# Zero matmuls ahead of the first load, a first load in halves, and a reordered first pair in an adaptive-norm FFN kernel with low-rank experts

## The reference

```python
W = weights[condition]                                  # (64 samples, 64, 64)
y = jnp.einsum('bct,bcd->bdt', x, W)                    # channels mixed per sample
logits = y @ gate_w.T                                   # 8 experts
w, sel = jax.lax.top_k(logits, 2); w = softmax(w)
result = y @ base_w.T + base_b                          # 1024 -> 1024
low    = y @ lora_A.T                                   # 8 experts of rank 16
result = result + 2.0 * sum_e(gate_e * low_e @ lora_B[e].T)
out = x + result
```

## Time and profile before

| what | value |
|---|---|
| median of the three runs | 504.84 us |
| the profiled execution's own time | 504.92 us |
| its span, first to last instruction | 502.8 us |
| PE busy | 489.8 us (97%) |
| DVE, ACT, POOL busy | 364.8, 380.7, 125.5 us |
| mean granted clock of PE | 0.997 |

### The profile page before, as it was taken

The page is one execution under the profiler, slowest core; times in us unless marked ns, Lnnn a source line. Parts: engine busy times, 40 slices in busy tenths (PEclk is TensorE's granted clock), DMA queues, the critical chain, the costliest instruction groups (busy, mean ns, idle before and its releaser), DMA issues.

```text
span 502.8 us, 8563 instructions
## 1 busy us (share of the span) xinstructions
PE 489.8 (97%) x2776; PEld 481.2 (96%) x2776; DVE 364.8 (73%) x768; ACT 380.7 (76%) x739; POOL 125.5 (25%) x111
## 2 busy tenths in 40 slices
PE   5979999999999999999999999999999999999997
PEld 5879999999999999999999999999999999999997
DVE  3987777877777877777877777877777877777654
ACT  4947887877887877887877887877887877887620
POOL 1240233321233320333311233321233321233110
PEclk9989999999999999999999999999999999999999
DMA  8812112222112222112222112222112222111112
GB/s 332 339 42 85 47 39 83 85 86 83 47 36 83 83 83 83 42 42 83 83 83 83 42 42 83 83 83 83 40 43 83 83 83 83 40 45 43 43 43 83
DMA packets 11105, 40.07 MB, mean 80 GB/s; under 512 B 1234, under 2 KB 1618, under 8 KB 11090
## 3 DMA queue, kind: packets, MB, share of 16 engines
q1 hardware_dynamic: 10946, 39.36, 21.6%
q10 hardware_dynamic: 144, 0.52, 0.3%
HBM read 23.10 MB, written 16.78 MB: 79 GB/s over the span
## 4 chain that ended last, share of the span: by engine, by line
PE 93%; DVE 3%; DMA 2%; ACT 1%; SPq 0%; issue 0%
PE acc L579 78%; PE acc L611 9%; PE mixed L599 6%; DMA w_raw<-in_proj_w 2%; DVE w_lo L408 2%; PE acc L605 1%; DVE ties L455 0%; ACT w_hi L308 0%; DVE x_parts L421 0%; DVE lb_lo L531 0%; DVE w_raw L429 0%; DVE y_lo L414 0%; SPq L201 0%; ACT cw_parts L362 0%; SPq L197 0%
## 5 line engine op out<-in xcount | busy, mean ns | idle before, releaser
L335 ACT COPY y_moved<-w_raw 32x256 f32<-32x256 f32 x480 | 194.2, 405 | 40.1 <-DVE w_raw L429 34.1
L579 PE MATMUL acc<-w_hi,y_hi 128*128 128x384 f32 (+1 forms) x768 | 182.8, 343 | 0.1
L579 PE MATMUL acc<-w_lo,y_hi 128*128 128x384 f32 (+1 forms) x768 | 179.9, 339 | 0.8 <-DVE w_lo L408 0.8
L579 PE MATMUL acc<-w_hi,y_lo 128*128 128x384 f32 (+1 forms) x768 | 179.6, 339 | 0.0
L268 POOL TENSOR_TENSOR w_raw<-x_sb,bias 128x1024 f32<-128x1024 f32 x32 | 77.1, 2410 | 350.9 <-DVE low L485 260.3
L579 PEld LDWEIGHTS acc<-w_hi,y_hi 128*128 128x128 f32 x768 | 136.0, 189 | 7.0 <-issue 0.4
L579 PEld LDWEIGHTS acc<-w_lo,y_hi 128*128 128x128 f32 x768 | 138.8, 188 | 1.9 <-DVE w_lo L408 1.8
L579 PEld LDWEIGHTS acc<-w_hi,y_lo 128*128 128x128 f32 x768 | 139.0, 188 | 0.1
L429 DVE TENSOR_TENSOR w_raw<-mixed,w_raw 64x1024 f32<-64x1024 f32 x60 | 73.0, 1216 | 40.5 <-ACT w_raw L327 40.1
L437 DVE STREAM_TRANSPOSE y_turned<-y_moved 128x512 f32<-128x512 f32 x60 | 39.2, 691 | 55.2 <-ACT y_moved L335 55.2
L421 DVE TENSOR_TENSOR x_parts<-x_sb,x_parts 64x1024 fp32r<-64x1024 f32 x60 | 74.0, 1234 | 1.9
(11 more groups left out here) (45 smaller groups left out, 240.1 us busy)
## 6 DMA issues: line engine op xcount, KB each, us to landing
x_sb<-in_x SPq DMA_DIRECT2D x32, 512.0 KB, 3.8
out<-w_raw SPq DMA_DIRECT2D x31, 512.0 KB, 2.9
w_raw<-in_proj_w SPq DMA_DIRECT2D x8, 580.0 KB, 9.6
cw<-in_cond_w ACTq DMA_DIRECT2D x1, 512.0 KB, 3.8
lb_raw<-in_lora_b SPq DMA_DIRECT2D x1, 512.0 KB, 14.4
bias<-in_base_b SPq DMA_DIRECT2D x1, 512.0 KB, 15.8
out<-w_raw SPq DMA_DIRECT2D x2, 192.0 KB, 1.9
out<-w_raw SPq DMA_DIRECT2D x1, 128.0 KB, 2.0
```

The source lines that it names most:

```text
L335: done = nc.scalar.copy(y_moved[q * SQ:(q + 1) * SQ, g, :, :], piece.rearrange("m (k q a) -> m q k a", q=QUARTERS, a=SQ)[:, q, :, :])
L579: return nc.tensor.matmul(acc[:, c % 2, b, 0:hi - lo], y_part[:, c % 2, k, :], w_part[:, k, lo:hi], start=(k == 0 and product == 0), stop= ...
```

## The change

Six edits. (1) POOL clears a tile `zeros`, and PE multiplies it with itself 8 times before it waits for x. (2) x of pair 0 is loaded in two halves with a semaphore each, and `mix_first(0, 0)` waits for the first half alone. (3) The register loads of the conditions of pairs 0 and 1 are made before the wait for `cw`; ACT rounds `cw` in halves as its first work, and the low part moves from POOL to DVE. (4) `w_high(0)` comes behind both `y_high_first` of pair 0 and covers 384 columns, DVE copies the other 776 (signal `w_first`). (5) In `first_step` the `w_lo` products run a block behind; in step 1 the mix of pair 2 moves from before k=0 to behind it, and its second half from behind k=1 to behind k=2; `lb_lo` moves from before the gates of pair 0 to behind `add_rest`. (6) POOL's `add_bias` in step c is that of pair c-1 instead of c, and the last is behind the steps.

The core of the diff:

```diff
-            load_x(0, 0)
+            sp.dma_start(x_sb[:, 0, 0:T // 2], x_pairs[0, :, 0:T // 2]).then_inc(x_first, 16)
+            sp.dma_start(x_sb[:, 0, T // 2:T], x_pairs[0, :, T // 2:T]).then_inc(x_in[0], 16)
...
@@ gpsimd
+            nc.gpsimd.memset(zeros[:, :], 0.0).then_inc(zeros_ready, 1)
...
-            pool.wait_ge(cw_hi_ready, 1)
-            nc.gpsimd.tensor_tensor(cw_parts[:, 1, :], cw[:, :], cw_parts[:, 0, :].bitcast(F32), ALU.subtract) \
-                .then_inc(cw_ready, 1)
-            pool.wait_ge(cw_ready, 1)
+            pool.wait_ge(cw_ready, 2)
             select(0, 2)
-            pool.wait_ge(w_ready, KT)
-            pool.wait_ge(lb_ready, 1)
             pool.wait_ge(bias_in, 16)
-            add_bias(0, 0)
             def step(j, c, ahead=True):
                 pool.wait_ge(low_ready, 4 * j + c)
-                add_bias(j, c)
+                add_bias(j, c - 1)
...
@@ scalar
-            w_high(0)
+            act.wait_ge(cw_in, 16)
+            for cols in CW_HALVES:
+                nc.scalar.copy(cw_parts[:, 0, cols], cw[:, cols]).then_inc(cw_hi_ready, 1)
             y_high_first(0, 0)
             y_high_first(0, 1)
+            w_high(0)
             w_high(1)
             w_high(2)
-            act.wait_ge(cw_in, 16)
-            nc.scalar.copy(cw_parts[:, 0, :], cw[:, :]).then_inc(cw_hi_ready, 1)
...
@@ vector
+            for i, cols in enumerate(CW_HALVES):
+                dve.wait_ge(cw_hi_ready, i + 1)
+                nc.vector.tensor_tensor(cw_parts[:, 1, cols], cw[:, cols], cw_parts[:, 0, cols].bitcast(F32),
+                                        ALU.subtract).then_inc(cw_ready, 1)
             y_low_first(0, 0)
+            dve.wait_ge(w_in[0], 16)
+            nc.vector.tensor_copy(w_hi[:, 0, BW:N], w_raw[:, 0, BW:N]).then_inc(w_first, 1)
...
@@ tensor, first_step
                 for k in range(KT):
                     pe.wait_ge(w_hi_ready, k + 1)
                     for b in range(3):
-                        project(0, k, b, 0)
-                    pe.wait_ge(w_ready, k + 1)
-                    for b in range(3):
-                        project(0, k, b, 1)
+                        if k == 0 and b == 1:
+                            pe.wait_ge(w_first, 1)
+                        project(0, k, b, 0, last=1)
...
+                        with_w_lo(0)
+                    if k >= 2:
+                        with_w_lo(k - 1)
+                with_w_lo(KT - 1).then_inc(proj_done, 1)
@@ tensor, step
-                if ahead:
+                if ahead and c >= 2:
                     mix(j, c + 1, 0)
...
-                    if k == 1 and ahead:
+                    if k == 0 and c == 1:
+                        mix(j, c + 1, 0)
+                    if k == (2 if c == 1 else 1) and ahead:
                         mix(j, c + 1, 1)
@@ tensor, start
-            pe.wait_ge(consts_ready, NE)
-            pe.wait_ge(x_in[0], 16)
+            pe.wait_ge(zeros_ready, 1)
+            for _ in range(WARM):
+                nc.tensor.matmul(acc[:, 1, 0, 0:P], zeros[:, :], zeros[:, :], start=True, stop=True)
+            pe.wait_ge(x_first, 16)
```

More of the change, by code:

```diff
@@ L85, in adaln_ffn_kernel @@
         ident = sb("ident", [P, P], F32)
+        zeros = sb("zeros", [P, P], F32)
         earlier = sb("earlier", [P, NE, NE], F32)
@@ L127, in adaln_ffn_kernel @@
         bias_in = sem("bias_in")
+        x_first = sem("x_first")
         x_in = [sem(f"x_in{i}") for i in range(4)]
@@ L134, in adaln_ffn_kernel @@
         lb_ready = sem("lb_ready")
+        zeros_ready = sem("zeros_ready")
         w_zero = sem("w_zero")
+        w_first = sem("w_first")
         first_lower = sem("first_lower")
@@ L190, in adaln_ffn_kernel @@
         LAST = PAIRS - 1
+        WARM = 8
+        CW_HALVES = (slice(0, CONDITIONS * CH // 2), slice(CONDITIONS * CH // 2, CONDITIONS * CH))
         @block.sync
@@ L245, in _ @@
                                     pattern=[[-1, P]], channel_multiplier=1).then_inc(consts_ready, 1)
[L247 to L251, removed]
             def select(j, c):
@@ L271, in _ @@
             pool.wait_ge(cond_in, 16)
+            lower = [pool.value_load(cond_sb[0:1, 2 * c:2 * c + 1], min_val=0, max_val=CONDITIONS - 1)
+                     for c in range(2)]
             pool.wait_ge(cw_in, 16)
             pool.wait_ge(w_zero, 1)
-            select_first(0)
-            select_first(1)
-            pool.wait_ge(cw_hi_ready, 1)
-            nc.gpsimd.tensor_tensor(cw_parts[:, 1, :], cw[:, :], cw_parts[:, 0, :].bitcast(F32), ALU.subtract) \
-                .then_inc(cw_ready, 1)
-            pool.wait_ge(cw_ready, 1)
+            for c in range(2):
+                nc.gpsimd.tensor_copy(w_pair[0:CH, c, 0:CH], cw[0:CH, bass.ds(lower[c] * CH, CH)]) \
+                    .then_inc(first_lower, 1)
+            pool.wait_ge(first_lower, 2)
+            pool.wait_ge(cw_ready, 2)
             select(0, 2)
-            pool.wait_ge(w_ready, KT)
-            pool.wait_ge(lb_ready, 1)
             pool.wait_ge(bias_in, 16)
-            add_bias(0, 0)
             def step(j, c, ahead=True):
                 pool.wait_ge(low_ready, 4 * j + c)
-                add_bias(j, c)
+                add_bias(j, c - 1)
                 if ahead:
                     select(j, c + 2)
-            for n in (1, 2, 3):
+            for n in (1, 2, 3, 4):
                 step(0, n)
             with pool.Fori(0, LOOPS) as j:
-                for u in (4, 5, 6, 7):
+                for u in (5, 6, 7, 8):
                     step(j, u)
-            for n in range(PAIRS - 4, PAIRS):
+            for n in range(PAIRS - 3, PAIRS):
                 step(0, n, ahead=(n + 2 < PAIRS))
+            add_bias(0, LAST)
         @block.scalar
@@ L307, in w_high @@
                 act.wait_ge(w_in[k], 16)
-                nc.scalar.copy(w_hi[:, k, :], w_raw[:, k, :]).then_inc(w_hi_ready, 1)
+                cols = slice(0, BW if k == 0 else N)
+                nc.scalar.copy(w_hi[:, k, cols], w_raw[:, k, cols]).then_inc(w_hi_ready, 1)
             def y_high_first(c, h):
@@ L510, in _ @@
             dve.wait_ge(cond_in, 16)
+            upper = [dve.value_load(cond_sb[0:1, 2 * c + 1:2 * c + 2], min_val=0, max_val=CONDITIONS - 1)
+                     for c in range(2)]
             dve.wait_ge(cw_in, 16)
@@ L513, in _ @@
             for c in range(2):
-                cond = dve.value_load(cond_sb[0:1, 2 * c + 1:2 * c + 2], min_val=0, max_val=CONDITIONS - 1)
-                nc.vector.tensor_copy(w_pair[CH:P, c, CH:P], cw[CH:P, bass.ds(cond * CH, CH)]).then_inc(first_upper, 1)
-            w_low(0)
+                nc.vector.tensor_copy(w_pair[CH:P, c, CH:P], cw[CH:P, bass.ds(upper[c] * CH, CH)]) \
+                    .then_inc(first_upper, 1)
+            for i, cols in enumerate(CW_HALVES):
+                dve.wait_ge(cw_hi_ready, i + 1)
+                nc.vector.tensor_tensor(cw_parts[:, 1, cols], cw[:, cols], cw_parts[:, 0, cols].bitcast(F32),
+                                        ALU.subtract).then_inc(cw_ready, 1)
             y_low_first(0, 0)
+            dve.wait_ge(w_in[0], 16)
+            nc.vector.tensor_copy(w_hi[:, 0, BW:N], w_raw[:, 0, BW:N]).then_inc(w_first, 1)
             y_low_first(0, 1)
-            for k in range(1, 4):
+            dve.wait_ge(w_first, 1)
+            for k in range(4):
                 w_low(k)
@@ L541, in step @@
                     add_rest(j, c + 1, 1)
+                if c == 1:
+                    dve.wait_ge(lb_hi_ready, 1)
+                    nc.vector.tensor_tensor(lb_lo[:, :], lb_raw[:, :], lb_hi[:, :].bitcast(F32), ALU.subtract) \
+                        .then_inc(lb_ready, 1)
                 if split:
@@ L574, in _, with project @@
             PRODUCTS = [(y_hi, w_hi), (y_hi, w_lo), (y_lo, w_hi)]
-            def project(c, k, b, product):
+            def project(c, k, b, product, last=2):
                 y_part, w_part = PRODUCTS[product]
@@ L579, in project @@
                 return nc.tensor.matmul(acc[:, c % 2, b, 0:hi - lo], y_part[:, c % 2, k, :], w_part[:, k, lo:hi],
-                                        start=(k == 0 and product == 0), stop=(k == KT - 1 and product == 2))
+                                        start=(k == 0 and product == 0), stop=(k == KT - 1 and product == last))
             def mix_first(c, h):
@@ L615, in first_step, with with_w_lo @@
             def first_step():
+                def with_w_lo(k):
+                    pe.wait_ge(w_ready, k + 1)
+                    for b in range(3):
+                        done = project(0, k, b, 1, last=1)
+                    return done
                 for k in range(KT):
@@ L627, in first_step @@
                     for b in range(3):
-                        done = project(0, k, b, 2)
+                        project(0, k, b, 2, last=1)
                     if k == 0:
@@ L693, in _ @@
             mix_first(0, 0)
+            pe.wait_ge(x_in[0], 16)
             mix_first(0, 1)
```

(1 more changed line is left out.)

4 lines of the change are left out of this document (removed).

## The result

| | median | runs | span of the profiled run |
|---|---|---|---|
| before | 504.95 us | 4 | 502.8 us |
| changed | 499.50 us (498.83 to 500.05) | 4 | 497.6 us |

The ratio is 0.9893, interval 0.9871 to 0.9915: 5.4 us faster. The forecast was 498.5 with a range of 497.1 to 500.7.

What follows compares the result with a forecast made beforehand. PE, busy 97% of the span, was taken as the bound, with at most 19 us to win. Gains of 2.3 + 4.1 = 6.4 us from 504.92 gave 498.5 us, own range 497.4 to 499.4, overall 497.1 to 500.7.

Steps and rivals of the forecast that it cites:

- Start: Edits 1 to 4, up to the first product: mix of pair 0 from 5.4 us, taking 1.95 instead of 3.54.
- The rival with the low clock: Mix of pair 0 stays at the low clock despite the zeros; gain 5.3 us, time 499.6, chance 0.18.
- The copy of 776 columns: DVE's share of weight block 0 before the first product: 0.85 us, costing 0.1 at most.
- First product: PE's first product of pair 0, forecast to start at 8.6 us, after ACT's w_hi of 384 columns ends at 8.5.
- The rival on splitting x: Halves of x delay the weights by at most 0.9 us, shifting DMA, ACT and DVE; time 499.4, chance 0.07.
- First step: Pair 0, with w_lo a block behind: ends at 23.35 us against 25.63, 2.3 us gained.
- Step 1 and 2: PE's 3.07 us wait in step 1 and its clock loss go: 5.0 less 0.9, so 4.1 us gained.
- The loss put in at 0.9: New lateness in steps 1 and 2, including a 0.5 us wait for lowT_lo; 0.9 us, bounds 0 and 2.
- The 5.0 us: What step 1 lost before the change by the wait and low clock: 20.14 us against 15.11.
- Bias a pair later: Edit 6 in steady steps: later loads of x and the extra add at the end cost nothing.

Runs made afterwards that it cites:

- x_whole: The changed kernel with x of pair 0 loaded in one transfer instead of two halves; 500.32 us, ratio 0.9919.
- repaired_whole: The kernel of repaired with x of pair 0 loaded in one transfer instead of two halves; 498.24 us, ratio 0.9878.
- bias_early: The changed kernel with POOL's bias additions back at their old places (pair c in step c); 500.58 us, ratio 0.9921.
- repaired: The changed kernel with weight block 0 rounded before pair 0's second y_high, x of pair 3 ahead of lb_raw, lowT_lo ahead of x_low in step 1; 499.24 us.
- after_again: The changed kernel run and profiled once more with nothing edited; 499.88 us, ratio 0.9903.

## Why the prediction was right, and where it was off

The measured 499.50 lies in the overall range, but just outside the 497.4 to 499.4 that the forecast gave itself, and beside two rivals, at 499.6 and 499.4. The time alone doesn't tell them apart; the profiles show that the stall went, as forecast, and that what both rivals describe, a low clock in the mix and late weights, happens as well. (The forecast's own range was put 0.2 too low: a loss of 0 to 2 us in place of 0.9 gives 497.6 to 499.6.) Step 2 was to start near 39 and started at 40.51.

*Start.* The mix came out, at 5.40 and with 2.05 us for 1.95. Its length was luck: the fast mix was taken as the rule, and is there in 4 of 10 profiles with zeros. The rival with the low clock was given 0.18 and is the commoner case; its 499.6 lies beside the medians of 499.5 and 499.9. The copy of 776 columns was put at 0.85 and took 0.61.

*First product, 8.6 forecast, 9.03 measured.* Here the sum was mis-sized: it took block 0's landing as unchanged, and it came 1.0 us later. ACT was free for it at 8.07, as forecast (8.05), so 0.3 us of this reached the first product; another 0.1 is the rounding of 384 columns, 0.51 us and not 0.4. The rival on splitting x named that cost, up to 0.9, at 0.07 and gave 499.4. The ten profiles with halves and the four without show that the halves, with the issue that they add, cost 30 to 80 GB/s in the 4 us around them. What that is worth in the kernel's time is not shown: whole transfers were 0.4 us slower in x_whole and 1.0 faster in repaired_whole, both with overlapping intervals. The Trainium skill's rule ("SBUF — State Buffer", "Summary: rules for kernel authors": one DMA, not several) was the better guide to the sign of what the loads did. The 2 us a transfer of its section "The DMA setup-cost knee" is not what is seen (block 0 lands 0.4 to 1.0 us later than before), nor does a second split add to it.

*First step, 2.3 us forecast, 25.63 - 23.89 = 1.7 measured*, mostly for that reason: 0.4 of the 0.5 us that pair 0 ended late is the late first product.

*Step 1 and 2, 4.1 us forecast, 3.5 measured* (5.19 - 1.74). The stall and the low clock went, as reasoned: in the kernel before `ties` on DVE, held by POOL's add, made 2.2 of the 3.07 us, and edit 6 alone moves step 3 by 3.5 us. It was not the only way, which the prediction did not see: bias_early has `ties` at 2.16 us and no wait of PE there, since `lb_lo` (1.2 us of DVE) and the stall of a `w_lo` (1.5 us) are out of the way of the gates and PE asks behind k=2. Which of these it needs was not tested apart. The loss put in at 0.9 was 1.6. (The 5.0 us that it is taken from are 0.16 too many: they run from a start in the timeline to one in the chain; in the timeline alone step 1 was 45.61 - 25.63 = 19.98 us.) ACT's `rest` began at 27.02 and not 25.5, behind the rounding of x of pair 3, and `lowT_lo` came at 35.54 and not 34.3. The wait for it (0.65) was the one forecast (0.5). That x landed at 24.9 instead of 22.4, more than the weights' 1.0 us; in x_whole, with block 0 only 0.2 us late, it still landed at 23.6, so halves are not the whole cause, and the rest stays open.

*Bias a pair later.* Nothing lost: 441.9 us behind step 3 in both.

Open is why halves of 2 KB rows are served more slowly, and whether zeros shift the median at all: the medians with zeros are 0.3 to 0.7 us lower in one pair of kernels and 0.2 us higher in the other (repaired), all within the intervals.

## What to carry to other kernels

An idle stretch of PE that brings the clock down costs more than itself (here 3.07 us of idle time and 1.5 us behind it, in 23 of 31 runs); look for what the late engine was doing, and whether a neighbour held it, before adding work to warm the clock. Put operations of VectorE with two inputs from SBUF and operations of GpSimd that read SBUF at different times. Take edits out as well as putting them in alone: two that remove the same stall each look like most of the gain. Ahead of a full load queue, splitting the first transfer can delay what is queued behind it by more than it wins.

## What the runs showed of the hardware that was not expected

The rise of PE's clock after an idle start is a lottery from one execution to the next: with the same 16 records on zeros from 1.05 us it came before 4.7 us in four profiles and only after the mix in six; in after_again products still ran slowly past 10.4. The mixes fall in two groups, of 2.0 and 3.8 us, with nothing between. The page's granted clock reads 1.00 in all of these stretches; only the length of the records shows the level.
